# A prefix sum of V on TensorE instead of on VectorE and DMA transposes, in a Taylor-attention plus ternary-FFN kernel

## The chip, the cores and the metric

The kernel runs on the eight cores of one Trainium2 chip. Each core gets one sample of the batch (2048 rows of 1024) and works alone; no data passes between cores. The metric is the device time in microseconds of the slowest core. PE is TensorE, DVE is VectorE, ACT is ScalarE, SP is the SyncE queue, which here issues the DMA transposes, and POOL is GpSimd.

## The reference, cut to what matters

```python
xn  = layernorm(x)                                  # [2048, 1024] per core
q, k = xn @ Wq.T, xn @ Wk.T                         # 16 heads x 16 features
v   = xn @ Wv.T                                     # 16 heads x 64
qf, kf = taylor_exp(q), taylor_exp(k)               # [1, x/2, x(x)x/(4 sqrt 2)]
A   = tril(qf @ kf.T)                               # per head, 2048 x 2048
y   = A @ v
y   = y * rsqrt(mean(y*y) + 1e-5) * g
out = x + y @ Wo.T + gelu(xn @ tern(W1).T + b1) @ tern(W2).T + b2
```

With s = q.k, an entry of A is 1 + s/4 + s²/32, which is (s/√32 + 4/√32)² + 0.5. The kernel squares and accumulates only the first term. The constant 0.5, under the causal mask, adds 0.5 times the running sum of V over the sequence to each row of y. This prefix sum is what the change touches.

## The kernel before, in words

One core's program runs in stages. First LayerNorm, while ACT sums the absolute values of W1 and W2 as they are loaded. Then the q, k and v projections on PE (L715), copied out of PSUM by ACT (L616). Then the prefix sum of V, then attention over eight pairs of heads, then the output projection, the ternary weights and the FFN.

**The prefix sum before.** V lies in `v_tm` with the sequence on partitions. SP transposes it by DMA into `vTc` (L215, sixteen transposes), so that the sequence runs along the free dimension. DVE scans it in place with 128 `tensor_tensor_scan` of 128x128 (L401), each tile starting from the last column of the one before. For each pair and each of 16 tiles of 128 rows SP transposes the piece back by DMA into `cumvT` (L230, 128 transposes in all). DVE adds 0.5 times that piece when it copies y out of PSUM into `y_tm` (L435).

**A pair's loop.** For pair p, PE first writes zeros into the four banks of `psY` (L761), each bank after DVE has copied the previous pair's y out of it. For m = 0 to 15, and for each of the two heads, PE computes scores in chunks of up to 512 columns into four buffers `psS` in turn (L778). Chunk i needs the buffer of chunk i-4. Every third chunk is turned by DVE into its square (L464, then L468), the other two by ACT (L649), both into `A_buf`. DVE masks the diagonal block (L479). PE accumulates `A_buf` times V into `psY` (L746, 128x64 results, each with its own weight load). It does so for m-1 after the scores of m. After m = 4, 8, 12 and at the end a bank is closed (L753) and DVE copies its four tiles out. There are 80 chunks in a pair.

**The head of a pair.** On DVE, from pair 1 on, two memsets of `qh_ext` rows (L445) stand ahead of the chunks; PE's first score waits for both. Behind them come the squares and sums of the previous pair's y (L411, L414) and, from pair 2 on, a reciprocal and sixteen scalings of the pair before that (L421, L427). Only then does DVE take its first chunk, which is chunk 2. Without it PE stops before chunk 6.

**The start of pair 0.** SP's program is in order: it waits for all transposes into `vTc` before it loads the first two heads of q into `qh_ext` (L221), and PE's first score waits for these. DVE's program is in order too: all 128 scans stand ahead of its first chunk.

Of the kernel before, what the change touches and what calls it, by code (L numbers as in the profile page):

```python
# [38 lines left out]
def build_program():  # L39
# [22 lines left out]
    xnT = at("xnT", [128, NT, KD, 128], BF16, 0)  # L62
    vTc = at("vTc", [128, NT, KD, 128], BF16, 32)
    w12_sb = at("w12_sb", [128, 32768], BF16, 32)
# [6 lines left out]
    ajunk = at("ajunk", [128, T], BF16, 72)  # L71
    cumvT = at("cumvT", [128, 2, NT, 128], BF16, 176)
    wv_bf = at("wv_bf", [128, KD, D], BF16, 48)
# [19 lines left out]
    A_buf = at("A_buf", [128, 4, T], BF16, 112)  # L93
    ones_scan = at("ones_scan", [128, T], BF16, 184)
    wk_bf = at("wk_bf", [128, KD, 256], BF16, 188)
# [32 lines left out]
    def S(name):  # L128
        return ctx.enter_context(nc.semaphore(name))
# [16 lines left out]
    sXN = S("sXN"); dXNT = DS("dXNT")  # L146
    sPQ = S("sPQ"); sPE = S("sPE"); dVT = DS("dVT"); sCUM = S("sCUM")
    sEXT = S("sEXT"); sSC = S("sSC"); sPOLY = S("sPOLY"); sPOLYV = S("sPOLYV"); sDM = S("sDM")
    sAV = S("sAV"); sYB = S("sYB"); sYE = S("sYE"); sYT = S("sYT")
    dCVT = DS("dCVT"); sQZ = S("sQZ")  # L150
    dP1L = DS("dP1L"); sP1R = S("sP1R"); sTHR = S("sTHR"); sZL = S("sZL")
# [45 lines left out]
    def sync_stream(e):  # L197
# [6 lines left out]
        for t in range(NT):  # L204
            e.wait_ge(sXN, t + 1)
            if t >= 2:
# [3 lines left out]
                                 transpose=True), t)  # L210
        for t in range(NT):
            e.wait_ge(sPE, 48 if t >= 8 else 33 + t)
            if t >= 2:
                dVT.wait_done(e, t - 2)
            dVT.inc(e.dma_start(out=vTc[:, t, :, :],  # L215
                                in_=blk(v_tm[:, t, :], KD), transpose=True), t)
        dVT.wait_all(e, NT)
        for h in (0, 1):
# [4 lines left out]
        for p in range(8):  # L223
            for t in range(NT):
                if p >= 2:
                    e.wait_ge(sYE, 16 * (p - 2) + t + 1)
                e.wait_ge(sCUM, 8 * (t + 1))
                if 16 * p + t >= 2:
                    dCVT.wait_done(e, 16 * p + t - 2)
                dCVT.inc(e.dma_start(out=cumvT[:, p % 2, t:t + 1, :],  # L230
                                     in_=vTc[:, t, p:p + 1, :],
                                     transpose=True), 16 * p + t)
            for h in (2 * p + 2, 2 * p + 3):
                if h < 16:
                    e.wait_ge(sSC, last_sc_of_pair[p])
                    e.wait_ge(sQZ, 2 * p - 1 if p >= 2 else 1)
                    r0 = 16 * (h % 8)
                    e.dma_start(out=qh_ext[r0:r0 + 16, h % 2, :],
                                in_=qT[r0:r0 + 16, h // 8, :]).then_inc(sEXT, 16)
            if p >= 3:  # L240
                pp = p - 3
                e.wait_ge(sRMc, NT * (pp + 1))
                e.wait_ge(sRMcS, NT * (pp + 1))
                if pp >= 2:
                    dYTT.wait_done(e, pp - 2)
                dYTT.inc(e.dma_start(out=blk(yT[:, pp, :], NT),
                                     in_=y_tm[:, pp % 4, :, :],
                                     transpose=True), pp)
# [95 lines left out]
    def vec_stream(e):  # L344
# [13 lines left out]
        pub(e.memset(ones1_bf[:], 1.0))  # L358
        pub(e.memset(zrow_bf[:], 0.0))
        pub(e.memset(cc(C_ONE), 1.0))  # L360
        pub(e.memset(consts[0:1, C_OR:C_OR + 128], 1.0))
        pub(e.memset(ones_scan[:], 1.0))
        pub(e.memset(cc(C_CBI), BI))
# [4 lines left out]
        pub(e.memset(cc(C_CZ), 0.0))  # L368
        pub(e.memset(cc(C_CO), 1.0))
        fence()  # L370
        for tp in range(0, NT, 2):
# [18 lines left out]
            for t in (tp, tp + 1):  # L390
                e.wait_ge(sLNrc, t + 1)
                e.tensor_scalar(xn_tm[:, t, :], u_sb[:, t % 2, :],
                                cc(C_RC + t), None, ALU.mult).then_inc(sXN, 1)
        for t in range(NT):
            dVT.wait_done(e, t)
            for c in range(KD):
                sl = vTc[:, t, c, :]
                init = 0.0 if t == 0 else vTc[:, t - 1, c, 127:128]
                if t > 0:
                    e.wait_ge(sCUM, 8 * (t - 1) + c + 1)  # L400
                e.tensor_tensor_scan(sl, sl, ones_scan[:, 0:128], init,  # L401
                                     ALU.add, ALU.mult).then_inc(sCUM, 1)
        pvk = [0]
# [26 lines left out]
        def evac_t(p, t):  # L430
            if t == 0 and p >= 4:
                dYTT.wait_done(e, p - 4)
            e.wait_ge(sYB, 4 * p + t // 4 + 1)
            dCVT.wait_done(e, 16 * p + t)
            e.scalar_tensor_tensor(  # L435
                y_tm[:, p % 4, t, :], cumvT[:, p % 2, t, :], 0.5,
                psY[:, 128 * t:128 * (t + 1)],
                ALU.mult, ALU.add).then_inc(sYE, 1)

# [253 lines left out]
    def ten_stream(e):  # L693
# [24 lines left out]
        e.wait_ge(sPE, 48)  # L718
        e.wait_ge(sCUM, 8)

# [36 lines left out]
        for p in range(8):  # L757
            for b in range(4):
                if p > 0:
                    e.wait_ge(sYE, 16 * (p - 1) + 4 * (b + 1))  # L760
                e.matmul(psY[:, 512 * b:512 * (b + 1)], zrow_bf[:],  # L761
                         v_tm[0:1, 0, 0:512], start=True, stop=False)
            for m in range(NT):
                chs = strip_chunks(m)
# [130 lines left out]
```

## Time and profile before

| | us |
|---|---|
| median of 2 runs | 1515.3 |
| lowest, highest | 1505.99, 1524.61 |
| the profiled execution, its time | 1505.63 |
| its span on core 0, the slowest | 1503.9 |
| spans of the other cores | 1483.6 to 1501.7 |

The profiled execution is read on core 0. Times in it count from the first instruction of that core; its span is 1.7 us shorter than the time of the execution. The stages on core 0 are: LayerNorm and weight sums to about 217 us, projections to 298 us, the wait for the prefix sum to about 326 us, the eight pairs to 773 us, and the rest to the end.

### The profile page before, as it was taken

How to read it: one execution, taken by the hardware profiler on the slowest of the kernel's cores; microseconds unless marked ns; L12 is line 12 of the kernel's file. 1: busy time of each engine (PE TensorE's matmuls, PEld its weight loads, DVE VectorE, ACT ScalarE, POOL GpSimd, SP SyncE). 2: the span in 40 equal slices, each digit the busy share in tenths (PEclk: the TensorE clock that was granted, in tenths of full speed). 3: DMA queues.
4: the chain of work that ended last, by engine and by line, in shares of the span. 5: the costliest groups of instructions: out<-in, count | busy, mean ns of one | idle time of the engine just before them, and what ended most of it. 6: DMA issues, size and time to landing. Idle time of an engine off the chain costs nothing.

```text
span 1503.9 us, 19832 instructions; the slowest of 8 cores (1483.6 to 1503.9 us)
## 1 busy us (share of the span) xinstructions
PE 925.5 (62%) x5528; PEld 433.0 (29%) x5608; DVE 597.4 (40%) x1406; ACT 528.8 (35%) x886; POOL 93.2 (6%) x155
## 2 busy tenths in 40 slices
PE   0000049936767657667543953888898506899995
PEld 0000014414334324334221321333343203344442
DVE  2222100687777777776762535222222100001000
ACT  1555333336657767667660211333333200000000
POOL 1111100000000000000001000111111100010010
PEclk9999999959879879779776986999999857999998
DMA  9878970330000010110217844545445564564662
GB/s 193 238 251 266 220 145 1 63 68 9 12 18 9 12 32 7 28 31 7 43 27 168 287 177 164 163 149 162 157 161 164 171 183 114 147 141 115 174 152 36
DMA packets 157670, 175.39 MB, mean 117 GB/s; under 512 B 77440, under 2 KB 128640, under 8 KB 153472
## 3 DMA queue, kind: packets, MB, share of 16 engines
q0 software_dynamic: 24928, 97.53, 23.6%
q1 hardware_dynamic: 132640, 76.60, 20.0%
q8 instruction: 52, 0.85, 0.2%
q14 instruction: 50, 0.41, 0.1%
HBM read 119.56 MB, written 41.94 MB: 107 GB/s over the span
## 4 chain that ended last, share of the span: by engine, by line
PE 32%; DMA 31%; DVE 18%; issue 11%; ACT 3%; POOL 1%; SPq 1%; DVEq 1%; another core or an unknown queue 0%; PEld 0%; POOLq 0%; ACTq 0%; PEldq 0%
DMA wst<-w2T 10%; PE psS L852 8%; PE psS L778 6%; DMA p1st<-w1T 6%; PE psS L715 5%; PE psY L852 5%; DMA xnT<-xn_tm 4%; DVE pv L464 4%; PE psY L746 4%; DMA hg_ts<-hg_scr 3%; DMA w_sb<-w2t_scr 3%; ACT A_buf L649 2%; PE psS L816 2%; PE psY L816 2%; DVE A_buf L468 2%
## 5 line engine op out<-in xcount | busy, mean ns | idle before, releaser
L649 ACT ACTIVATE A_buf<-psS,consts 128x512 bf16<-128x512 f32 (+3 forms) x427 | 277.7, 712 | 174.3 <-PE psS L778 146.2
L830 PE MATMUL psS<-xnT,w_sb 128*128 128x512 bf16 x1024 | 232.7, 386 | 69.1 <-DVE w_sb L525 39.7
L778 PE MATMUL psS<-qh_ext,kT 128*128 128x512 bf16 (+3 forms) x593 | 181.1, 385 | 149.1 <-DVE A_buf L468 73.3
L852 PE MATMUL psS<-w_sb,hg_ts 128*128 128x512 bf16 x501 | 114.6, 387 | 75.4 <-DMA hg_ts<-hg_scr 71.6
L830 PEld LDWEIGHTS psS<-xnT,w_sb 128*128 128x128 bf16 x1024 | 99.4, 99 | 202.3 <-issue 93.1
L464 DVE TENSOR_SCALAR pv<-psS 128x512 bf16<-128x512 f32 (+3 forms) x213 | 129.5, 608 | 59.9 <-PE psS L778 50.8
L715 PE MATMUL psS<-xnT,wq_bf 128*128 128x512 bf16 x64 | 21.9, 515 | 206.7 <-DMA xnT<-xn_tm 206.7
L682 ACT ACTIVATE hgst<-psS,consts 128x512 bf16<-128x512 f32 x128 | 85.5, 686 | 172.7 <-DMA hg_scr<-hgst 91.4
L778 PEld LDWEIGHTS psS<-qh_ext,kT 128*128 128x128 bf16 x640 | 62.1, 99 | 249.5 <-issue 236.3
L746 PE MATMUL psY<-v_tm,A_buf 128*128 128x64 bf16 x2176 | 119.2, 192 | 18.8 <-DVE A_buf L479 5.6
L746 PEld LDWEIGHTS psY<-v_tm,A_buf 128*128 128x128 bf16 x2176 | 98.7, 97 | 45.7 <-issue 31.4
L852 PE MATMUL psY<-w_sb,hg_ts 128*128 128x512 bf16 x502 | 111.3, 379 | 0.5
L561 DVE TENSOR_SCALAR jw2a<-wst,consts 128x1024 bf16<-128x1024 f32 x32 | 24.1, 753 | 193.2 <-DMA wst<-w2T 193.2
L589 ACT ACTIVATE ajunk<-p1st 128x2048 bf16<-128x2048 f32 x32 | 61.1, 1910 | 109.1 <-DMA p1st<-w1T 55.1
L468 DVE TENSOR_TENSOR A_buf<-pv 128x512 bf16<-128x512 bf16 (+3 forms) x213 | 82.0, 385 | 22.6 <-DVE pv L464 0.6
L852 PEld LDWEIGHTS psS<-w_sb,hg_ts 128*128 128x128 bf16 x512 | 50.5, 100 | 139.5 <-issue 83.1
L551 DVE TENSOR_TENSOR out_sb<-psS,x_re 128x512 f32<-128x512 f32 x16 | 11.1, 692 | 178.4 <-PE psS L852 178.4
L401 DVE TENSOR_TENSOR_SCAN vTc<-vTc,ones_scan 128x128 bf16<-128x128 bf16 x128 | 47.8, 456 | 77.6 <-DMA vTc<-v_tm 77.6
L715 PEld LDWEIGHTS psS<-xnT,wq_bf 128*128 128x128 bf16 x64 | 7.5, 121 | 220.5 <-issue 217.3
L852 PEld LDWEIGHTS psY<-w_sb,hg_ts 128*128 128x128 bf16 x512 | 50.0, 98 | 60.5
L715 PE MATMUL psS<-wv_bf,xnT 128*128 128x512 bf16 x250 | 54.9, 379 | 0.3
L551 DVE TENSOR_TENSOR out_sb<-psY,x_re 128x512 f32<-128x512 f32 x16 | 11.1, 692 | 99.4 <-PE psY L852 99.4
(96 smaller groups left out, 707.3 us busy)
## 6 DMA issues: line engine op xcount, KB each, us to landing
p1st<-w1T POOLq DMA_DIRECT2D x16, 1024.0 KB, 7.9
p1st<-w2T POOLq DMA_DIRECT2D x16, 1024.0 KB, 8.2
wst<-w1T POOLq DMA_DIRECT2D x16, 1024.0 KB, 8.6
wst<-w2T POOLq DMA_DIRECT2D x32, 512.0 KB, 4.7
hg_scr<-hgst SPq DMA_DIRECT2D x128, 128.0 KB, 2.4
hg_ts<-hg_scr SPq DMA_DIRECT2D x32, 512.0 KB, 9.1
x_roll<-x SPq DMA_DIRECT2D x16, 512.0 KB, 6.0
out<-out_sb SPq DMA_DIRECT2D x16, 512.0 KB, 6.0
```

The source lines that it names most:

```text
L401: e.tensor_tensor_scan(sl, sl, ones_scan[:, 0:128], init, ALU.add, ALU.mult).then_inc(sCUM, 1)
L464: pub(e.tensor_scalar(pv[:, slot, 0:w], psS[idx % 4][:, 0:w], SC, BI, ALU.mult, ALU.add))
L468: e.tensor_tensor(A_buf[:, gs % 4, t0:t0 + w], pv[:, slot, 0:w], pv[:, slot, 0:w], ALU.mult).then_inc(sPOLYV, 1)
L589: e.activation(ajunk[:], p1st[:, i % 2, :], AF.Abs, accum_out=cc(col)).then_inc(sP1R, 1)
L649: e.activation(A_buf[:, gs % 4, t0:t0 + w], psS[idx % 4][:, 0:w], AF.Square, bias=cc(C_CBI), scale=cc(C_CSC)).then_inc(sPOLY, 1)
L682: e.activation(hgst[:, i % 2, :], ps[:], AF.Gelu, bias=consts[:, C_B1 + j:C_B1 + j + 1]).then_inc(sHGs, 1)
L715: mm = e.matmul(ps[:], lhsT, rhs, start=(c == 0), stop=(c == KD - 1))
L746: e.matmul(psY[:, 128 * t + 64 * hi:128 * t + 64 * hi + 64], A_buf[:, gs % 4, 128 * t:128 * (t + 1)], v_tm[:, m, h * E:(h + 1) * E], start ...
L778: e.matmul(psS[idx % 4][:, 0:w], kT[:, h // 8, m * 128:(m + 1) * 128], qh_ext[:, hi, t0:t0 + w], start=True, stop=True).then_inc(sSC, 1)
L816: e.matmul(ps, yT[:, c, t * 128:(t + 1) * 128], wo_bf[:, c, dh * 512:(dh + 1) * 512], start=(c == 0), stop=False)
L830: mm = e.matmul(ps[:], w12_sb[:, c * FF + j * 128:c * FF + j * 128 + 128], xnT[:, 4 * tb:4 * tb + 4, c, :], start=(c == 0), stop=(c == KD ...
L852: mm = e.matmul(ps, hg_ts[:, k % 2, j, (ts % 2) * 128:(ts % 2) * 128 + 128], w12_sb[:, j * D + dh * 512:j * D + (dh + 1) * 512], start=(j ...
```

## The change

The prefix sum moves to PE. Two constant 128x128 matrices are made: `oneh`, all 0.5, and `tril05`, the mask times 0.5. At the head of each pair, behind the zeros and ahead of the first score, PE accumulates into `psY`, for each tile mm_ of V and each row tile t from mm_ to 15, one matmul of 128 columns: with `tril05` for t = mm_, with `oneh` for t above it. That is 136 matmuls for each pair and 1088 in all. The transposes into `vTc`, the scans, and the transposes into `cumvT` are gone. DVE's copy out of `psY` becomes a plain `tensor_copy`. SP loads the first two heads of q once the eight q projections are copied out. PE's wait for the first scans becomes one for `tril05`. In the diff, renamed semaphores and tile declarations are left out.

```diff
@@ sync_stream
-        for t in range(NT):
-            e.wait_ge(sPE, 48 if t >= 8 else 33 + t)
-            if t >= 2:
-                dVT.wait_done(e, t - 2)
-            dVT.inc(e.dma_start(out=vTc[:, t, :, :],
-                                in_=blk(v_tm[:, t, :], KD), transpose=True), t)
-        dVT.wait_all(e, NT)
+        e.wait_ge(sPE, 8)
         for h in (0, 1):
             r0 = 16 * (h % 8)
             e.wait_ge(sQZ, 1)
             e.dma_start(out=qh_ext[r0:r0 + 16, h % 2, :],
                         in_=qT[r0:r0 + 16, h // 8, :]).then_inc(sEXT, 16)
         for p in range(8):
-            for t in range(NT):
-                if p >= 2:
-                    e.wait_ge(sYE, 16 * (p - 2) + t + 1)
-                e.wait_ge(sCUM, 8 * (t + 1))
-                if 16 * p + t >= 2:
-                    dCVT.wait_done(e, 16 * p + t - 2)
-                dCVT.inc(e.dma_start(out=cumvT[:, p % 2, t:t + 1, :],
-                                     in_=vTc[:, t, p:p + 1, :],
-                                     transpose=True), 16 * p + t)
             for h in (2 * p + 2, 2 * p + 3):
@@ vec_stream
+        pub(e.memset(oneh[:], 0.5))
-        pub(e.memset(ones_scan[:], 1.0))
+        fence()
+        e.tensor_scalar(tril05[:], tril_bf[:], 0.5, None,
+                        ALU.mult).then_inc(sVM, 1)
@@
-        for t in range(NT):
-            dVT.wait_done(e, t)
-            for c in range(KD):
-                sl = vTc[:, t, c, :]
-                init = 0.0 if t == 0 else vTc[:, t - 1, c, 127:128]
-                if t > 0:
-                    e.wait_ge(sCUM, 8 * (t - 1) + c + 1)
-                e.tensor_tensor_scan(sl, sl, ones_scan[:, 0:128], init,
-                                     ALU.add, ALU.mult).then_inc(sCUM, 1)
@@ evac_t
             e.wait_ge(sYB, 4 * p + t // 4 + 1)
-            dCVT.wait_done(e, 16 * p + t)
-            e.scalar_tensor_tensor(
-                y_tm[:, p % 4, t, :], cumvT[:, p % 2, t, :], 0.5,
-                psY[:, 128 * t:128 * (t + 1)],
-                ALU.mult, ALU.add).then_inc(sYE, 1)
+            e.tensor_copy(y_tm[:, p % 4, t, :],
+                          psY[:, 128 * t:128 * (t + 1)]).then_inc(sYE, 1)
@@ ten_stream
         e.wait_ge(sPE, 48)
-        e.wait_ge(sCUM, 8)
+        e.wait_ge(sVM, 1)
@@ the head of each pair, behind the zeros
+            for mm_ in range(NT):
+                for t in range(mm_, NT):
+                    e.matmul(psY[:, 128 * t:128 * (t + 1)],
+                             tril05[:] if t == mm_ else oneh[:],
+                             v_tm[:, mm_, 128 * p:128 * (p + 1)],
+                             start=False, stop=False)
```

## Rows read from the trace of the kernel before

**Rows 1.** The page: engines' busy us; one group: busy us, mean ns, idle before.

```profile
PE 925.5 (62%) x5528; PEld 433.0 (29%) x5608; DVE 597.4 (40%) x1406; ACT 528.8 (35%) x886; POOL 93.2 (6%) x155
...
L746 PE MATMUL psY<-v_tm,A_buf 128*128 128x64 bf16 x2176 | 119.2, 192 | 18.8 <-DVE A_buf L479 5.6
```

**Rows 2.** Waits of PE: engine line <- waited for: us, times, longest us.

```profile
PE psS L778 <- DVE A_buf L468: 73.3, 67, 8.2
...
PE psS L778 <- DVE qh_ext L445: 30.6, 7, 4.4
...
PE psS L778 <- DMA qh_ext<-qT: 16.6, 1, 16.6
```

**Rows 3.** Windows, pair 7: engines' busy us (x), granted clock, DMA share, GB/s.

```profile
715.30:773.00 57.70, 36.55 (x351) 20.34 (x356) 44.13 (x122) 35.51 (x59) 0.00 (x0) 0.85 0.13 25
```

**Rows 4.** Timeline around pair 0's start: start us, us, engine, line, tiles, [idle before].

```profile
295.94 0.59 ACT L616 CAST v_tm<-psS 128x512 bf16<-128x512 f32 x1 [1.14 <-PE psS L715]
297.67 0.59 ACT L616 CAST v_tm<-psS 128x512 bf16<-128x512 f32 x1 [1.14 <-PE psS L715]
...
298.51 1.02 PE L761 MATMUL psY<-v_tm,zrow_bf 1*128 1x512 bf16 x4 [0.93 <-DVE vTc L401]
...
301.77 24.16 DVE L401 TENSOR_TENSOR_SCAN vTc<-vTc,ones_scan 128x128 bf16<-128x128 bf16 x64 [2.53 <-DMA vTc<-v_tm]
...
325.85 0.67 DVE L464 TENSOR_SCALAR pv<-psS 128x512 bf16<-128x512 f32 x1
...
327.87 2.79 ACT L649 ACTIVATE A_buf<-psS,consts 128x512 bf16<-128x512 f32 x4 [8.24 <-PE psS L778]
...
330.15 0.69 DVE L464 TENSOR_SCALAR pv<-psS 128x512 bf16<-128x512 f32 x1 [0.51 <-PE psS L778]
```

**Rows 5.** Timeline at the head of pair 3.

```profile
482.84 1.98 PE L761 MATMUL psY<-v_tm,zrow_bf 1*128 1x512 bf16 x4
...
484.58 1.76 DVE L445 MEMSET qh_ext<- 32x2048 bf16 x1 [0.48 <-DVE y_tm L435]
...
489.22 2.48 PE L778 MATMUL psS<-qh_ext,kT 128*128 128x512 bf16 x5 [4.40 <-DVE qh_ext L445]
...
495.35 0.69 DVE L464 TENSOR_SCALAR pv<-psS 128x512 bf16<-128x512 f32 x1
...
496.72 0.59 PE L778 MATMUL psS<-qh_ext,kT 128*128 128x512 bf16 x1 [5.02 <-DVE A_buf L468]
...
497.40 4.02 ACT L649 ACTIVATE A_buf<-psS,consts 128x512 bf16<-128x512 f32 x6 [5.09 <-PE psS L778]
```

**Rows 6.** Timeline at the head of pair 1.

```profile
370.53 1.99 PE L761 MATMUL psY<-v_tm,zrow_bf 1*128 1x512 bf16 x4
...
379.96 0.68 DVE L464 TENSOR_SCALAR pv<-psS 128x512 bf16<-128x512 f32 x1
...
382.00 2.68 ACT L649 ACTIVATE A_buf<-psS,consts 128x512 bf16<-128x512 f32 x4 [3.03 <-PE psS L778]
```

**Rows 7.** Windows: clock after the projections, then from two starts of dense PE work.

```profile
298.30:301.00 2.70, 1.02 (x4) 0.30 (x4) 0.94 (x3) 0.00 (x0) 0.00 (x0) 0.94 0.52 98
...
440.60:447.60 7.00, 6.28 (x46) 2.64 (x46) 4.93 (x13) 5.60 (x9) 0.00 (x0) 0.76 0.12 24
...
554.30:561.30 7.00, 6.63 (x45) 2.60 (x45) 5.24 (x12) 5.54 (x8) 0.00 (x0) 0.59 0.13 27
```

**Rows 8.** Timeline of PE and its weight loads in pair 7, full clock.

```profile
754.69 0.38 PE L778 MATMUL psS<-qh_ext,kT 128*128 128x512 bf16 x1
...
758.11 0.69 PE L746 MATMUL psY<-v_tm,A_buf 128*128 128x64 bf16 x18
...
757.89 0.78 PEld L746 LDWEIGHTS psY<-v_tm,A_buf 128*128 128x128 bf16 x18
```

**Rows 9.** Groups by line and shape: busy us, mean ns, idle before.

```profile
L435 DVE SCALAR_TENSOR_TENSOR y_tm<-cumvT,psY 128x128 bf16<-128x128 bf16 x128 | 28.2, 282 | 13.0 <-PE psY L753 13.0
...
L464 DVE TENSOR_SCALAR pv<-psS 128x128 bf16<-128x128 f32 x21 | 6.1, 290 | 7.6 <-PE psS L778 7.5
```

## What the change will do to the time

> **What bounds the kernel now.** I read the page first. PE is busy in 62% of the span [rows 1], so no engine bounds the whole; each stage has to be asked what it waits for. The list of PE's waits shows three that belong to attention: for the q rows of `qh_ext` by DMA, once, 16.6 us; for the memsets of `qh_ext` at seven pair heads, 30.6 us; for squares from DVE, 73.3 us in 67 waits [rows 2]. Then the timeline of the start of pair 0. ACT begins to copy the last projection out at 297.67 us. PE writes zeros at once, from 298.51, and then has nothing to do: DVE scans, and its first chunk is at 325.85 [rows 4]. The 27 us from 298.5 on are the price of the prefix sum where it stands now. Within pairs it is nearly free: no wait of DVE for `cumvT` appears among its waits.
>
> The next place is the head of a later pair, since the change puts its work there. At pair 3 the zeros begin at 482.84 and last 1.98 us. PE then waits for the memsets that start at 484.58, issues five scores from 489.22, and waits 5.02 us for DVE, until 496.72. DVE is at its own head work up to 495.35, when it takes its first chunk [rows 5]. So between 484.8 and 495.35 PE has 10.6 us in which it does 2.5 us of scores. This idle time recurs in six pairs (2 to 7; from the first memset to the first chunk all have 10.8 us, to 0.1). Pair 1 has no scaling work and DVE is back at 379.96, with the zeros issued from 370.53 for 1.99 us, so 7.5 us after them [rows 6]. The last pair has 57.7 us and ends at 773 [rows 3]. Last I read the granted clock, because PE's new work falls there.
>
> **Part 1, what is removed: the wait before pair 0.** After the change PE goes from the projections into the zeros (298.51 to about 299.4) and into 136 matmuls. In the 2.7 us behind the projections the clock is 0.94 of full in the mean [rows 7], though PE stands idle in the second half of them; with no idle gap I take the full 2.4 GHz. What does one 128-column matmul with its own load cost? No row has them in a stream. Below it are 18 matmuls of 64 columns, each with its load, in 0.69 us of which the last one's own 0.19 us [rows 1] goes off: 0.50/17 = 29 ns [rows 8]. Above it are the projections, eight 512-column matmuls for each of ACT's copies, which start at 295.94 and 297.67: 1.73/8 = 216 ns [rows 4]. On the line between, 128 columns cost 29 + (216-29) x 64/448 = 56 ns, and 136 of them 7.6 us. The upper bound is a load that hides behind nothing. Loads stream at (0.78-0.10)/17 = 40 ns [rows 8], so 96 ns and 13.1 us. I take 56, since the 64-column row hides a whole load in 29 ns.
>
> A rule that speaks against this stands in the Trainium skill, TensorE: Matmul & The Clock Gate, section Back-to-back issue gap: a sustained stream of load and matmul pairs needs about 81 ns for each 128-column matmul. By it the block would be 11.0 us at full clock, and the whole sum, worked out as below, about +4 us instead of a gain. The row of 29 ns for 64 columns disagrees in kind, and no row here shows 128 columns.
>
> So the block ends at 299.4 + 7.6 = 307.0. The first score takes 0.38 us at full clock [rows 8] and reaches ACT 0.1 us later; ACT's four first units last 2.79 us as they do at 327.87 [rows 4]; ACT is ready for its fifth at 310.3. Before, it began the fifth at 327.87. That is 17.6 us earlier. DVE would start at 307.9 instead of 325.85, 17.9 us earlier. The smaller counts: **-17.6 us**.
>
> **Part 2, what is added at the heads of pairs 2 to 7.** The block starts when the zeros are through, 484.8 at pair 3. Here the clock stands at half. From nine starts of dense PE work (eight pairs and the output projection) I took windows of 7 us; their mean clocks are 0.59 to 0.76 [rows 7]. With c us at half clock the mean is 1 - c/14, so c is 3.4 to 5.7 us, 4.4 in the mean. At half clock 128 columns take twice the 53 ns, 107 ns. In 4.4 us that is 41 matmuls; the other 95 take 5.3 us. The block lasts 9.7 us (9.2 to 10.4 for the ends of c; 14.5 if the clock never rises) and ends at 494.5. PE's third score then ends at 494.5 + 2 x 0.216 + 0.38 and is with DVE at 495.4. DVE is free at 495.35, so nothing is lost there. ACT loses its head start. It gets its first chunk at 495.0, is through four at 497.8, and begins the fifth 0.4 us after the 497.40 of before [rows 5]. Against that PE comes out of the block at full clock. Before, a pair's first 3.4 to 5.7 us of scores ran at half, each taking 0.59 against 0.38 us [rows 5, 8]. About three of them lie in the chain from square to score to square in that time: 0.6 us back. Net -0.2 us for each of six pairs: **-1.2 us**. The 10.6 us are the cover; what the block has over 9.7 us costs its full length in all seven later pairs.
>
> **Pair 1.** The block starts at 372.45 and ends at 382.1. ACT begins its fifth unit at 385.4 instead of 382.00 [rows 6]: +3.4, less 0.6: **+2.8 us**. Pair 0 gets the same 0.6 us for a clock that is up where it was at half: **-0.6 us**.
>
> **Part 3, what is smaller.** The copy out of `psY` was 282 ns; the nearest plain op on PSUM of that shape is 290 ns [rows 9], so +1 us over 128 of them at most, mostly beside other work. I take 0. The waits for `cumvT` were never last. The `ones_scan` memset goes (2048 columns take 1.76 us [rows 5]) and two small ops come. It stood ahead of LayerNorm, a stage whose chain is the loading of W1 and W2 and ACT's sums behind it. I take 0, with -1.8 as the bound. SP's queue loses 144 transposes. The `qh_ext` loads of later pairs and `yT` wait for scores and for ACT, not for the queue. The first two q rows now leave SP during the projections. All behind 773 us starts from the last copies of pair 7 and moves with them.
>
> **Sum:** -17.6 - 0.6 + 2.8 - 1.2 = -16.6 us. From the profiled execution's 1505.6 that is **1489 us**. The median of the two runs is 1515.3, 10 us above that execution; I forecast for an execution like the profiled one. About 2% is what can be told from no change here, so -1.1% counts as within it.
>
> **The rivals.**
>
> *The clock pays more (faster).* If the clock rises soon, counted from the zeros at 482.84, c from the block's start is about 2.4 us, the block 8.7 us, and ACT's lag of 0.4 us is gone. If DVE's wait for a half-clock score in that stretch is gone as well (0.5 us [rows 4]), each of eight pairs gives about 0.9 us more: -7, so 1482 us. For it: PE was busy through the zeros. Against it: the units of ACT follow each other without gaps there, so it may be ACT that paces.
>
> *Loads do not hide.* A matmul then costs up to 96 ns. Halfway, at 76 ns, the block has 11.6 us at the heads (1.9 over) and 10.3 at pair 0 (2.7 over): 7 x 1.9 + 2.7 = +16, so 1505. At 96 ns it has 13.5 and 13.1 us: 7 x 3.8 + 5.5 = +32, so 1521. For it: no row shows this shape. Against it: the 64-column row. By the Trainium skill's rule above, this rival would stand at 1509.
>
> *The clock stays at half through the block (slower than before).* The block has 14.5 us at pairs 1 to 7, scores start cold, ACT begins its fifth unit at 484.8 + 14.5 + 0.7 + 2.8 = 502.8 instead of 497.4, 5.4 us late, six times; pair 1 is 8.4 late; with -17.6 that is +23, so 1529 us. It decides from a block of about 12 us on, where seven times the excess eats the gain. For it: half clock at every head now. Against it: all nine dense starts rose within 5.7 us.
>
> **How the numbers follow.** Forecast 0.62 (own range 1483 to 1497), the faster rival 0.18, loads 0.10, clock 0.06, the rest 0.04. The time is the forecast's, 1489. Down to 1476 and up to 1510 leaves out the upper half of the loads rival, the clock rival and part of the rest, under 2 in 10. Faster by over 2% needs more than the faster rival, or runs of before as long as the longer of the two shown: 0.12. Slower by over 2% needs 1536 and thus more than either slow rival: 0.03. Within 2%: 0.85.
>
> **What the new profile would show.** The block's matmuls at about 56 ns spacing at full clock and 107 at half; pair 0's first DVE chunk near 308; the block's end near 10 us after the zeros; PE's wait for `qh_ext` memsets gone; pairs 2 to 7 as long as before within 1 us and pair 1 about 3 us longer; pair 7's end near 756. I am wrong if the spacing is over 70 ns, if the clock stays at half through a block, or if the pairs' bodies change length for another reason.

## The result and the profile after

| | before | after |
|---|---|---|
| median, us | 1513.2 (10 runs) | 1492.5 (11 runs) |
| lowest, highest | 1504.9, 1540.3 | 1489.1, 1504.5 |
| span of core 0 in the profiled execution | 1503.9 | 1492.7 |
| from ACT's last projection copy to the last four copies of y, core 0 | 475.20 | 457.76 |

The ratio of the two kernels is 0.988, with a 95% interval of 0.984 to 0.993: 1.2% faster, some 18 us, and within 2%. In some executions one die shows a lower granted clock; the ratio leaves those out, and the medians do not. The forecast was 1489 us, 1.1% faster, for an execution like the profiled one; that one took 1494.5 us after, against 1505.6 before.

The span of the one profiled execution fell by 11.2 us, the attention stretch in it by 17.4. The rest is not the change's. From these last copies of y on, core 0 needs 731.0 us before (1503.9 - 772.87) and 735.7 after (1492.7 - 756.97); over all eight cores this tail, which the change doesn't touch, has 727.6 us in the mean before and 728.2 after. What lies ahead of the stretch has 291.5 and 291.8 us. So the attention stretch of core 0 is what I compare from here on, unless the text names other cores. It repeats well: over the eight cores it is 474.7 to 476.2 us before and 456.7 to 458.4 after, 475.3 and 457.7 in the mean.

The next table cuts this stretch where DVE starts the last four copies of each pair's y (L435, later L412; one row in the timelines of core 0). "First" runs from ACT's last projection copy to the end of pair 0.

| kernel | first | 1 | 2 | 3 | 4 | 5 | 6 | 7 | sum |
|---|---|---|---|---|---|---|---|---|---|
| before | 73.2 | 56.1 | 56.2 | 57.6 | 59.2 | 55.7 | 58.0 | 59.1 | 475.2 |
| after | 55.0 | 58.2 | 56.1 | 57.7 | 59.1 | 56.2 | 56.8 | 58.8 | 457.8 |
| e1_no_block | 47.8 | 56.2 | 56.1 | 57.9 | 59.3 | 56.2 | 57.3 | 60.0 | 450.8 |
| e2_double_block | 64.5 | 66.2 | 62.4 | 65.5 | 66.3 | 62.6 | 65.2 | 66.1 | 518.8 |
| e3_spread | 50.1 | 58.5 | 59.3 | 60.7 | 61.2 | 59.0 | 59.5 | 62.2 | 470.4 |
| e4_before_plus_heads | 73.2 | 58.5 | 56.0 | 57.2 | 58.5 | 55.6 | 58.6 | 59.5 | 477.1 |
| e5_pair0_spread | 50.3 | 57.8 | 56.1 | 57.9 | 58.8 | 55.3 | 56.8 | 58.7 | 451.7 |
| e6_pool_memset | 55.0 | 58.3 | 55.9 | 56.5 | 58.1 | 55.7 | 56.3 | 58.1 | 453.9 |
| e7_pool_memset_no_block | 47.6 | 52.0 | 52.5 | 52.9 | 54.7 | 52.0 | 53.1 | 54.6 | 419.5 |
| e8_pool_part_spread | 49.0 | 55.1 | 52.1 | 54.5 | 55.8 | 52.7 | 53.4 | 55.3 | 427.8 |
| e9_half_zero_block | 53.4 | 56.4 | 56.6 | 57.4 | 59.2 | 55.6 | 57.0 | 59.1 | 454.7 |
| e10_pool_k4 | 50.1 | 52.9 | 52.2 | 52.8 | 54.7 | 52.4 | 53.4 | 54.9 | 423.4 |
| e11_pool_spread_all | 49.1 | 54.9 | 54.9 | 55.7 | 57.1 | 55.3 | 55.7 | 56.6 | 439.2 |

After against before: -18.2 in the first stretch, +2.1 in pair 1, -1.3 in pairs 2 to 7 together, -17.4 in all. Now the lines behind each.

**The start of pair 0**, from the timeline of the kernel after (start us, us, engine, line, tiles, idle before it). It answers [rows 4].

```profile
299.21 0.59 ACT L591 CAST v_tm<-psS 128x512 bf16<-128x512 f32 x1 [1.14 <-PE psS L690]
...
300.05 1.02 PE L736 MATMUL psY<-v_tm,zrow_bf 1*128 1x512 bf16 x4 [0.93 <-ACT v_tm L591]
...
301.00 0.23 PE L740 MATMUL psY<-v_tm,tril 128*128 128x128 bf16 x1
...
308.55 0.22 PE L740 MATMUL psY<-v_tm,tril 128*128 128x128 bf16 x1
...
309.08 6.70 ACT L624 ACTIVATE A_buf<-psS,consts 128x512 bf16<-128x512 f32 x10 [9.28 <-remote]
...
309.52 0.69 DVE L439 TENSOR_SCALAR pv<-psS 128x512 bf16<-128x512 f32 x1 [107.26 <-PE psS L759]
```

The last projection copy starts at 299.21 here, 1.5 us later than before, so I count from it. (The trace calls `tril05` `tril`.) The zeros follow, then the block (L740) from 301.00; its last matmul starts at 308.55. That is 7.55 us for 135 steps, 55.9 ns each, at full clock. DVE takes its first chunk 10.3 us after the last projection copy; before it was 28.2 us (325.85 - 297.67).

**The head of pair 3**, which answers [rows 5]:

```profile
469.86 1.76 DVE L420 MEMSET qh_ext<- 32x2048 bf16 x1 [0.48 <-DVE y_tm L412]
...
470.03 0.29 PE L740 MATMUL psY<-v_tm,tril 128*128 128x128 bf16 x1
...
471.71 0.31 PE L740 MATMUL psY<-v_tm,tril 128*128 128x128 bf16 x1
...
479.04 0.22 PE L740 MATMUL psY<-v_tm,tril 128*128 128x128 bf16 x1
...
479.31 0.81 PE L759 MATMUL psS<-qh_ext,kT 128*128 128x512 bf16 x3
...
479.57 2.79 ACT L624 ACTIVATE A_buf<-psS,consts 128x512 bf16<-128x512 f32 x4 [8.72 <-remote]
...
480.63 0.69 DVE L439 TENSOR_SCALAR pv<-psS 128x512 bf16<-128x512 f32 x1
...
482.83 3.35 ACT L624 ACTIVATE A_buf<-psS,consts 128x512 bf16<-128x512 f32 x5 [0.47 <-PE psS L759]
```

The first sixteen matmuls of the block take 1.68 us (470.03 to 471.71), 105 ns each, at half clock. The last one starts at 479.04, so the block has 9.0 us plus the last one's time, and ACT has the first score at 479.57. DVE's first chunk comes 10.77 us after the memset's start, to the hundredth what [rows 5] show (495.35 - 484.58). PE's wait for the memsets, which end at 473.8, has gone; the block lies over them.

**The head of pair 1**, which answers [rows 6]:

```profile
355.45 1.76 DVE L420 MEMSET qh_ext<- 32x2048 bf16 x1 [0.36 <-DVE y_tm L412]
...
355.74 0.29 PE L740 MATMUL psY<-v_tm,tril 128*128 128x128 bf16 x1
...
365.53 0.22 PE L740 MATMUL psY<-v_tm,tril 128*128 128x128 bf16 x1
...
366.08 0.69 DVE L439 TENSOR_SCALAR pv<-psS 128x512 bf16<-128x512 f32 x1 [2.74 <-remote]
...
367.92 4.70 ACT L624 ACTIVATE A_buf<-psS,consts 128x512 bf16<-128x512 f32 x7 [0.19 <-PE psS L759]
```

Here the block ends too late. DVE's first chunk comes 10.63 us after the memset's start, against 7.81 before (379.96 - 372.15).

**What PE still waits for** (engine line <- waited for: us, times, longest us), against [rows 2]:

```profile
PE psS L759 <- DVE A_buf L443: 36.4, 73, 2.1
...
PE psS L759 <- ACT A_buf L624: 20.2, 65, 0.6
```

The waits for the q rows (16.6 us) and for the memsets (30.6) are gone, and that for DVE's squares is halved, from 73.3 to 36.4 us. That for ACT's grew from 13.9 to 20.2. So PE waits some 78 us less. Only 17 us of them became time; in the attention stretch PE is busy for 365.7 us where it was 306.1, and these 60 us are the block's matmuls.

**The groups of the page by line and shape** (busy us, mean ns, idle before), against [rows 1, 9]:

```profile
L740 PE MATMUL psY<-v_tm,oneh 128*128 128x128 bf16 x960 | 76.0, 246 | 0.0
...
L740 PE MATMUL psY<-v_tm,tril 128*128 128x128 bf16 x128 | 28.6, 234 | 0.0
...
L412 DVE CAST y_tm<-psY 128x128 bf16<-128x128 f32 x128 | 28.2, 283 | 11.9 <-PE psY L728 11.9
...
L361 DVE TENSOR_REDUCE consts<-x_roll 128x1 f32<-128x1024 f32 x16 | 18.8, 1211 | 1.0 <-DMA x_roll<-x 1.0
```

The plain copy out of PSUM (L412) has 283 ns where the one with the added tile had 282. The first LayerNorm operation (L361) starts 1.9 us earlier than before, at 9.49 us against 11.37, and the second then waits 1.0 us for x to land. Up to the last projection copy nothing of this is left that shows, as the means above say (291.5 and 291.8 us).

### The profile page after: what moved, and what is told of

Read it like the earlier page. It is cut to its first block, busy times and chain, and to the rows that moved or that the text cites. A ratio compares the mean times of both kernels' runs of the same rounds, so it can differ in the third digit from the quotient of the medians.

```text
span 1492.7 us, 21092 instructions; the slowest of 8 cores (1461.5 to 1492.7 us)
## 1 busy us (share of the span) xinstructions
PE 982.0 (66%) x6615; PEld 504.5 (34%) x6696; DVE 548.2 (37%) x1279; ACT 527.1 (35%) x886; POOL 93.5 (6%) x155
## 4 chain that ended last, share of the span: by engine, by line
DMA 34%; PE 29%; DVE 15%; issue 9%; ACT 4%; another core or an unknown queue 2%; SPq 2%; POOL 1%; PEld 1%; DVEq 1%; PEldq 0%; ACTq 0%; POOLq 0%
DMA wst<-w2T 11%; PE psS L833 8%; DMA hg_ts<-hg_scr 6%; DMA p1st<-w1T 6%; PE psS L690 5%; PE psS L759 5%; DMA xnT<-xn_tm 5%; DVE pv L439 4%; PE psY L721 4%; DMA w_sb<-w2t_scr 3%; ACT A_buf L624 3%; PE psS L797 2%; PE psY L797 2%; DVE A_buf L443 2%
## 5 line engine op out<-in xcount | busy, mean ns | idle before, releaser
L811 PE MATMUL psS<-xnT,w_sb 128*128 128x512 bf16 x1024 | 228.4, 381 | 80.3 <-ACT hgst L657 41.4
L759 PE MATMUL psS<-qh_ext,kT 128*128 128x512 bf16 (+3 forms) x592 | 165.2, 348 | 72.6 <-DVE A_buf L443 36.4
L721 PEld LDWEIGHTS psY<-v_tm,A_buf 128*128 128x128 bf16 x2176 | 97.9, 96 | 45.4 <-issue 30.6
L740 PE MATMUL psY<-v_tm,oneh 128*128 128x128 bf16 x960 | 76.0, 246 | 0.0
L740 PEld LDWEIGHTS psY<-v_tm,oneh 128*128 128x128 bf16 x960 | 72.7, 113 | 0.0
L833 PEld LDWEIGHTS psY<-w_sb,hg_ts 128*128 128x128 bf16 x512 | 50.1, 98 | 60.4
L690 PE MATMUL psS<-wv_bf,xnT 128*128 128x512 bf16 x250 | 54.9, 379 | 0.3
```

Of the source, the lines that this page charges most:

```text
L690: mm = e.matmul(ps[:], lhsT, rhs, start=(c == 0), stop=(c == KD - 1))
L721: e.matmul(psY[:, 128 * t + 64 * hi:128 * t + 64 * hi + 64], A_buf[:, gs % 4, 128 * t:128 * (t + 1)], v_tm[:, m, h * E:(h + 1) * E], start ...
L740: e.matmul(psY[:, 128 * t:128 * (t + 1)], tril05[:] if t == mm_ else oneh[:], v_tm[:, mm_, 128 * p:128 * (p + 1)], start=False, stop=False)
L759: e.matmul(psS[idx % 4][:, 0:w], kT[:, h // 8, m * 128:(m + 1) * 128], qh_ext[:, hi, t0:t0 + w], start=True, stop=True).then_inc(sSC, 1)
L811: mm = e.matmul(ps[:], w12_sb[:, c * FF + j * 128:c * FF + j * 128 + 128], xnT[:, 4 * tb:4 * tb + 4, c, :], start=(c == 0), stop=(c == KD ...
L833: mm = e.matmul(ps, hg_ts[:, k % 2, j, (ts % 2) * 128:(ts % 2) * 128 + 128], w12_sb[:, j * D + dh * 512:j * D + (dh + 1) * 512], start=(j ...
```

## The experiments

The theory: the gain is the wait before pair 0, and it pays the block's 7.6 us there in full; the block costs about 2 us at pair 1 (the forecast had 2.8, this is from the result), and in pairs 2 to 7 it lies under DVE's own work at the head, with almost nothing to spare. The rivals: the block costs time at every head; or the pairs' bodies have slack that takes up a late start; or pairs 2 to 7 stay equal because the removed transposes give back what the block takes.

### The block taken away

```diff
-            for mm_ in range(NT):
-                for t in range(mm_, NT):
-                    e.matmul(psY[:, 128 * t:128 * (t + 1)], ...)
```

> The changed kernel without its 136 matmuls at the head of each pair; the constant 0.5 term is left out of the output. My theory (the block is on the path at pair 0 with its full 7.6 us and at pair 1 with about 2 us, and under DVE's head work in pairs 2 to 7): against the changed kernel the stretch from ACT's last projection copy to pair 1's memset is 7.6 us shorter, pair 1 is about 2 us shorter, pairs 2 to 7 are the same within 0.5 us each, and the whole is about 10 us shorter. Rival (PE's time is missed at every head, since ACT starts its first chunk 5 us later than in the kernel before): pairs 2 to 7 are each at least 2 us shorter and the whole at least 20 us.

Against the kernel after, the first stretch is 7.2 us shorter and pair 1 2.0 us, as the theory has it. Pairs 2 to 7 are not shorter but 2.2 us longer together. So the whole is 7.0 us shorter, not 10. The rival is refuted: the heads of pairs 2 to 7 lose 0.9 us by the block, all six together, where it asked for 2 us or more each. The theory misses what the block gives back, 3.1 us in the bodies, 2.2 net. In e1 DVE's first chunk comes as before and ACT starts 5 us earlier than in the kernel after, so what differs must be in the bodies, and the granted clock there differs. First e1's windows of 10 us from DVE's first chunk in pairs 1 and 2, then the kernel after's for pairs 1 and 3 (busy us of the engines, the granted clock, DMA share, GB/s):

```profile
350.12:360.12 10.00, 7.90 (x49) 3.21 (x50) 7.65 (x19) 6.90 (x11) 0.00 (x0) 0.61 0.00 1
...
409.43:419.43 10.00, 7.74 (x50) 3.01 (x50) 7.69 (x19) 7.24 (x11) 0.00 (x0) 0.67 0.00 1
```

```profile
366.08:376.08 10.00, 7.02 (x52) 3.02 (x51) 7.96 (x18) 8.60 (x13) 0.00 (x0) 1.00 0.01 2
...
480.63:490.63 10.00, 7.45 (x51) 3.07 (x51) 7.38 (x19) 8.43 (x14) 0.00 (x0) 0.83 0.00 1
```

Without the block the clock in these 10 us is 0.61 to 0.75 of full over the seven pairs, with it 0.83 to 1.00. Whether this is the cause was tried in e9, and is read from the eight cores behind it.

### The block twice

```diff
+            for mm_ in range(NT):
+                for t in range(mm_, NT):
+                    e.matmul(psY[:, 128 * t:128 * (t + 1)],
+                             zlhs[:],
+                             v_tm[:, mm_, 128 * p:128 * (p + 1)],
+                             start=False, stop=False)
```

> The changed kernel with the block issued twice, the second time with weights of zeros, which add nothing. Theory (the block fills the cover of pairs 2 to 7 to within a microsecond, so everything beyond it counts in full): +7.6 us at pair 0 and +7.6 us at each of pairs 1 to 7, as the second block runs at full clock; 61 us in all. Rival (the bodies of the pairs have slack that takes up a late start): under 40 us in all.

61.0 us longer in the attention stretch (518.8 - 457.8), and the theory said 61. That the sum agrees so well is in part luck: the first stretch has 9.5 more, where 7.6 were expected (the last section shows where the clock fell there), and the seven others 6.4 to 8.4 each, 7.4 in the mean. The timeline of the head of its pair 3:

```profile
490.93 1.76 DVE L420 MEMSET qh_ext<- 32x2048 bf16 x1 [0.48 <-DVE y_tm L412]
...
501.34 7.76 PE L747 MATMUL psY<-v_tm,zlhs 128*128 128x128 bf16 x136
...
508.94 1.03 PE L766 MATMUL psS<-qh_ext,kT 128*128 128x512 bf16 x4
...
509.86 0.69 DVE L439 TENSOR_SCALAR pv<-psS 128x512 bf16<-128x512 f32 x1 [8.07 <-PE psS L766]
```

The zero-weight block (L747) runs for 7.76 us from 501.34, and DVE, done with its own head work, has its first chunk only at 509.86, 18.9 us after the memset's start instead of 10.8. There is next to no slack behind the head: DVE's first chunk comes 7.4 us later in the mean of pairs 2 to 7, and their bodies are only 0.2 us shorter each.

### The block's matmuls in the m loop

```diff
+                if m >= khead:            # khead = 0
+                    prefix(e, p, m)       # the matmuls of tile m of V
                 if m > 0:
                     emit_av(e, p, m - 1)
```

> The changed kernel with the same matmuls spread: those of tile m of V follow the scores of m instead of standing at the pair's head. Theory (the bodies are paced by the handing over between PE, ACT and DVE and PE stands idle in a fifth of them, but heads of pairs 2 to 7 gain nothing as DVE sets them): pair 0 is about 7.6 us shorter less some 3 us for the body, pair 1 about the same, pairs 2 to 7 each 1 to 4 us longer; the whole 5 to 15 us longer. Rival (bodies have room for all of it): pair 0 7.6 us and pair 1 2 us shorter, the rest equal, the whole 10 us shorter.

12.6 us longer, in the range of the theory: 4.9 us shorter in the first stretch, 0.2 longer in pair 1, 17.3 longer in pairs 2 to 7. The heads gain nothing (DVE's first chunk as in e1), and the 7.6 us of matmuls cost a body 2.5 us (e3 against e1 in pairs 1 to 7: 17.3/7). So, by the block's price at full clock, two thirds of the spread work fall into PE's gaps; the rival, that all of it does, is refuted.

### What is added, without what is removed

```diff
+            for mm_ in range(NT if p >= 1 else 0):
+                ...                        # zlhs weights, as in e2
```

> The kernel before, with a block of 136 matmuls whose weights are zeros (they add nothing) at the heads of pairs 1 to 7: the added part of the change alone, without what it removes. Theory: pair 1 is 2 us longer, pairs 2 to 7 together within 2 us of before, the stretch before pair 1 unchanged; about +1 us in all. Rival (the gain in pairs 2 to 7 that offsets the block comes from the transposes and their waits being gone): pairs 2 to 7 are each 0.5 us or more longer, and the whole is 5 us or more longer.

In the kernel before, the block at the heads of pairs 1 to 7 costs 2.4 us in pair 1 and -0.5 us in pairs 2 to 7 together, 1.9 us in all. The transposes and the added operand of the copy are still there, so their absence is not what offsets the block. Core 0 is the least favourable core here: in its pairs 6 and 7 the clock in the first 10 us from DVE's first chunk is 0.66, and they are 0.5 us longer than before, while on most other cores it is at full there. Over the eight cores the attention stretch is 475.3 us in the mean, with this block and without: +1.9 in pair 1, -1.7 in pairs 2 to 7, -0.1 ahead of them. So what is added costs nothing net, and what is removed gives the whole 17.6 us (475.3 - 457.7).

### The block spread in pair 0 only

```diff
+            khead = 0 if p == 0 else NT
```

> The changed kernel with pair 0's matmuls spread over its m loop as in e3_spread and the block kept at the heads of pairs 1 to 7. Theory (a block costs its length where nothing covers it, and spreading costs about 3 us of body): the stretch up to pair 1's memset is 4.9 us shorter, as e3 had it (51.3 against 56.2), all other pairs as in the changed kernel; the whole about 5 us shorter than the changed kernel. Rival (e3's short first stretch was paid by pair 1): pair 1 is 2 us or more longer than in the changed kernel.

4.7 us shorter in the first stretch (50.3) and 6.1 in all; pair 1 didn't pay for it (57.8 against 58.2). The ratio to the kernel before is 0.986 with an interval of 0.978 to 0.995, which overlaps that of the kernel after; the gain over it is read from the stretch, not from these.

### The cover taken away

```diff
 (DVE, head of the pair)
-                for hs in (0, 1):
-                    e.wait_ge(sSC, last_sc_of_pair[p - 1])
-                    e.memset(qh_ext[b0:b0 + 32, hs, :], 0.0).then_inc(sQZ, 1)
 (GpSimd)
+        for p in range(1, 8):
+            b0 = 32 * ((p - 1) % 4)
+            for hs in (0, 1):
+                e.wait_ge(sSC, last_sc_of_pair[p - 1])
+                e.memset(qh_ext[b0:b0 + 32, hs, :], 0.0).then_inc(sQZ, 1)
```

> The changed kernel with the two memsets of qh_ext at each pair's head moved from DVE to GpSimd. Theory (in pairs 2 to 7 the block lies under DVE's head work of 10.8 us, 3.9 us of which are these memsets, and becomes the limit when they go): DVE is free 3.9 us earlier but gets its first chunk only 0.5 to 1.5 us earlier, since the block ends when it did; the whole 3 to 8 us shorter than the changed kernel, pair 1 the same. Rival (the block is not what DVE would wait for next): DVE takes its first chunk 3 us or more earlier in each of pairs 2 to 7, 20 us in all.

> As e6_pool_memset, without the block, so that the constant 0.5 term is left out of the output. Theory: without the block nothing stands between the earlier DVE and its chunks; pairs 1 to 7 are each 3 to 3.9 us shorter than in e1_no_block, 21 to 27 us in all. Together with e6 this prices the block where its cover is gone: about 3 us for each of pairs 2 to 7 and over 5 us at pair 1, where it costs 0 and 2 us now. Rival (ACT or the row loads hold the head instead): less than 2 us a pair.

e6 is 3.9 us shorter than the kernel after, as the theory has it. DVE's first chunk comes 0.2 to 0.7 us earlier in pairs 2 to 7, 0.4 in the mean, so the block is what it waits for, and the rival is refuted. e7 is 31.2 us shorter than e1. The head of pair 3 in e6, where GpSimd's memsets run from 468.69 and DVE's last four copies of y from 470.70:

```profile
468.69 3.54 POOL L295 MEMSET qh_ext<- 32x2048 bf16 x2 [52.42 <-PE psS L760]
...
470.70 0.88 DVE L417 CAST y_tm<-psY 128x128 bf16<-128x128 f32 x4 [1.08 <-PE psY L729]
...
476.26 2.43 DVE L410 TENSOR_SCALAR y_tm<-y_tm,rinv 128x64 bf16<-128x64 bf16 x16
...
482.20 0.69 DVE L440 TENSOR_SCALAR pv<-psS 128x512 bf16<-128x512 f32 x1 [3.51 <-PE psS L760]
```

DVE is through with its scalings at 478.7 and takes its first chunk 3.5 us after that. And the same head in e7:

```profile
441.22 3.54 POOL L295 MEMSET qh_ext<- 32x2048 bf16 x2 [49.05 <-PE psS L754]
...
443.25 0.88 DVE L417 CAST y_tm<-psY 128x128 bf16<-128x128 f32 x4 [1.08 <-PE psY L729]
...
445.51 2.48 PE L754 MATMUL psS<-qh_ext,kT 128*128 128x512 bf16 x5 [0.66 <-issue]
...
448.80 2.43 DVE L410 TENSOR_SCALAR y_tm<-y_tm,rinv 128x64 bf16<-128x64 bf16 x16
...
451.14 0.68 DVE L440 TENSOR_SCALAR pv<-psS 128x512 bf16<-128x512 f32 x1
```

Now the scores begin at 445.51, and DVE's first chunk follows its scalings at once, 7.9 us after the last four copies began, against 12.1 in e1. With the cover gone the block costs 3.2 to 3.7 us in each of pairs 2 to 7 (e6 against e7) and 6.3 in pair 1, where it cost -0.4 and 2.0 us with it. At the heads alone it is 3.6 to 4.2 us in pairs 2 to 7, about the 3.9 us of memsets that went, and the bodies give some 0.5 us back. So the block was hidden by DVE's head work; it was not small in itself. The theory's figure for e7, 21 to 27 us, was low. The heads gained 4.0 to 4.2 us each, 29 us in all: besides the two memsets (3.5 us) the gaps ahead of them went (0.48 and 0.38 us). The other 2 us lie mostly in the bodies and stay unexplained.

### Both kernels beaten: the block cut to the cover

```diff
+            khead = 0 if p == 0 else 6     # e10: 0, then 2 for pair 1 and 4 for the others
+            for mm_ in range(khead):
+                prefix(e, p, mm_)
```

with GpSimd's memsets as in e6.

> GpSimd memsets as in e6; pair 0's prefix matmuls spread over its m loop; in pairs 1 to 7 those of V's tiles 0 to 5 (81 of 136) at the head and the other 55 in the m loop. Theory: the head block then lasts about 6.6 us, as long as DVE's head work without the memsets; each of pairs 2 to 7 gains about 3 us at the head and gives back 1.2 us in its body (3 us for 136 spread matmuls in e3), pair 0 gains 4.9 us; the whole 14 to 20 us shorter than the changed kernel. Rival (spread matmuls hurt where bodies start earlier and are denser): under 8 us shorter.

> e8_pool_part_spread with fewer matmuls at the head: V's tiles 0 and 1 (31 matmuls) in pair 1, 0 to 3 (58) in pairs 2 to 7, all others in the m loop. Theory (in e8 DVE still gets its first chunk 0.4 to 1.6 us after it is free, 3.1 us in pair 1): pair 1 is 2 us shorter, pairs 2 to 7 each 0 to 1 us shorter at the head less 0.5 us for the 23 more in the body; the whole 0 to 4 us shorter than e8. Rival (with a shorter block the clock is at half where the chunks begin and the body pays): 2 us or more longer than e8.

> GpSimd memsets and all prefix matmuls in the m loop, none at the head. Theory (matmuls in the head's cover are free, those in the body cost about 3 us for 136, as e3 had it against e1): against e7_pool_memset_no_block each pair is about 3 us longer, so the attention stretch is 20 to 25 us longer than e7's 419.5 and 10 to 17 us longer than e8's 427.8. Rival (e8 shows spreading to be nearly free once the head is short): within 6 us of e8.

| kernel | attention stretch, us | median, us | ratio to before, 95% interval |
|---|---|---|---|
| after | 457.8 | 1492.5 | 0.988 (0.984 to 0.993) |
| e8_pool_part_spread | 427.8 | 1458.5 | 0.970 (0.966 to 0.975) |
| e10_pool_k4 | 423.4 | 1459.9 | 0.971 (0.968 to 0.975) |
| e11_pool_spread_all | 439.2 | 1470.7, one run | |

e8 is 30 us shorter than the kernel after, where I expected 14 to 20, and 3.0% faster than the kernel before. Of the 30 us, 6.0 are pair 0's, whose matmuls are spread. The head of its pair 3:

```profile
442.73 0.88 DVE L417 CAST y_tm<-psY 128x128 bf16<-128x128 f32 x4 [0.85 <-PE psY L736]
...
448.29 2.43 DVE L410 TENSOR_SCALAR y_tm<-y_tm,rinv 128x64 bf16<-128x64 bf16 x16
...
451.55 0.81 PE L764 MATMUL psS<-qh_ext,kT 128*128 128x512 bf16 x3
...
452.26 0.69 DVE L440 TENSOR_SCALAR pv<-psS 128x512 bf16<-128x512 f32 x1 [1.54 <-PE psS L764]
```

DVE's first chunk comes 1.5 us after its scalings end and 9.5 us after the last four copies began; the kernel after needed 12.1. Over pairs 1 to 7 the heads gain 24.7 us and the pairs 24.0, so the bodies are 0.1 us longer each than in the kernel after. Against e6, which has the same memsets on GpSimd and nothing spread, they are 0.3 us longer each: that is the price of the 55 spread matmuls, where I had allowed 1.2 us. e10 removes what is left at the heads (DVE's first chunk at 7.9 us again, as without any block) and has 4.4 us less in the stretch, a little more than expected; in the medians, taken on another chip, the two can't be told apart. e11 shows that the part at the head is what pays: with none there, the stretch is 19.7 us longer than in e7 (20 to 25 expected) and 11.4 us longer than in e8, and its rival is refuted.

### The clock or ACT's start

```diff
-            for mm_ in range(NT):
+            for mm_ in range(5):           # zlhs weights: 70 matmuls
```

> The changed kernel with its block replaced by 70 matmuls with weights of zeros (tiles 0 to 4 of V), so that the constant 0.5 term is left out; it tells the clock from ACT's head start. e1_no_block was 1 us longer in pairs 2 to 6 and 1.1 us in pair 7 than the changed kernel, although its ACT starts 5 us earlier. Theory (the block brings the clock up before the chunks begin, which is worth some 0.6 us a pair): the short block of about 6 us ends as the scores of e1 would begin, ACT keeps most of its start, the clock in the first 10 us from DVE's first chunk is above 0.9, and pairs 2 to 7 together are 2 to 5 us shorter than in e1. Rival (the difference is nothing of the clock's): pairs 2 to 7 as in e1 within 1 us.

Inconclusive. Pairs 2 to 7 are together 1.9 us shorter than in e1 (344.9 against 346.8) on core 0, between what the two theories said, and 0.6 us shorter in the mean of the eight cores. And the condition didn't come about: the clock in the first 10 us is 0.66 to 0.83, since PE waits again behind the short block. The window of pair 2:

```profile
422.19:432.19 10.00, 7.66 (x48) 3.18 (x50) 7.52 (x19) 7.03 (x11) 0.00 (x0) 0.66 0.01 2
```

What e9 leaves open, the eight cores of one profile settle: they run the same program, and the clock falls at different times on them. Take pair 3 of the kernel after. On cores 0, 1, 2 and 6 the clock is at half for 3.4 of the first 10 us from DVE's first chunk, and the body lasts 45.4 to 45.5 us. On cores 3, 5 and 7 it is at half for 6.8 of them, and the body lasts 46.4 to 46.5 us. On all seven DVE's first chunk comes 12.1 us after the last four copies began, and ACT begins its fifth unit at the same point to 0.01 us. The whole body of pair 3 on core 0, then the first 10 us and the whole body on core 3:

```profile
480.63:526.14 45.51, 34.21 (x348) 19.99 (x353) 31.16 (x97) 36.02 (x59) 0.00 (x0) 0.94 0.02 4
...
474.75:484.75 10.00, 7.88 (x49) 3.47 (x48) 6.75 (x17) 7.65 (x13) 0.00 (x0) 0.66 0.00 1
474.75:521.15 46.40, 35.81 (x353) 20.63 (x353) 31.14 (x98) 35.95 (x59) 0.00 (x0) 0.89 0.02 4
```

So with the head as it was, more time at half clock makes this body 1.0 us longer. The means of the eight cores over pairs 2 to 7 say the same between kernels:

| kernel | clock in the first 10 us | the six heads, us | the six bodies, us |
|---|---|---|---|
| before | 0.70 | 72.5 | 273.5 |
| e4, before plus the block | 0.94 | 73.2 | 271.1 |
| e1, after without the block | 0.69 | 72.6 | 273.4 |
| e9, 70 matmuls at the head | 0.74 | 72.6 | 272.8 |
| after | 0.94 | 73.2 | 271.3 |
| e7, as e6 without the block | 0.70 | 47.4 | 272.3 |
| e6, memsets on GpSimd | 1.00 | 71.0 | 269.9 |

Of two kernels that differ by the block alone (before and e4, e1 and after, e7 and e6), the one with it has the six bodies 2.1 to 2.4 us shorter, some 0.4 us a pair.

## Why the prediction was right, step by step

**The matmul's price** was the widest unknown, 56 to 96 ns from rows of 64 and 512 columns. It measured 55.9 ns; a load hides behind 128 columns at full clock. The line between two shapes on either side was good to 0.2 ns (it gives 55.7 before rounding). The rule of the Trainium skill (TensorE: Matmul & The Clock Gate, Back-to-back issue gap), 81 ns, doesn't hold here.

**Part 1, -17.6 and -0.6 us** at pair 0: -18.2 us measured. DVE's first chunk comes 17.9 us earlier, to the tenth the figure that I had for DVE, and the body is 0.4 us shorter. e1 shows its two terms: the wait that was removed gives 25.4 us (73.2 - 47.8) and the block takes 7.2 back.

**Part 2, pairs 2 to 7, -1.2 us:** measured -1.3, and -1.5 in the mean of the eight cores. The overlap is as I had it; the close agreement is in part luck, since the two terms were both too large. The block's 9.7 us were right: it lasts 9.2 us at pair 3 and 9.2 to 10.5 over pairs 1 to 7, 9.9 in the mean. DVE's first chunk is unchanged in four pairs and late in the two with the longest blocks, by 0.8 us in pair 5 (10.5 us) and by 0.1 in pair 7 (10.4), +0.9 in all. So the cover ends where I had put it, and the pairs stand on its edge. (I gave all six the same 10.8 us from the first memset to the first chunk; pair 5 has 10.6.) For ACT I had a lag of 0.4 us, and its fifth unit at pair 3 is 0.15 us late. For the clock I had 0.6 us back in each body, and it is 0.4. Which scores give it back is not shown: that it is three half-clock scores at the start was a guess. In pair 3 the clock even fell to half again from 483.4 us on, after 0.8 us in which PE waited, so that pair had little of it.

**Pair 1, +2.8 us:** measured +2.1; the head is 2.8 later and the body 0.7 shorter. The step was wrong in a detail. I wrote that DVE's first chunk is chunk 2 in every pair and that ACT has four units ahead of it. Every third chunk is DVE's by a count that runs on over pairs of 80 chunks, so this holds for pairs 0, 3 and 6; in pair 1 it is the very first chunk. The timeline shows it: DVE at 366.08 is ahead of ACT. So the row at 382.00 [rows 6], which I took for ACT's fifth unit, is its third. The error cost little, since what counts is when the block ends.

**Part 3, zeros:** the copy has 283 ns against 282. The shorter DVE work ahead of LayerNorm and SP's shorter queue moved nothing that shows, as said.

**The rivals.** Loads that don't hide: no, 55.9 ns. The clock at half through the whole block: no, at pair 3 it rose about 3 us after the block's start; what a block beyond the cover costs, e2 shows. The clock pays more: the stretch came out 0.8 us beyond my sum, where this rival asked for 7, and the block at the heads had 9.2 us at the least on core 0, not 8.7.

**The cover** of 10.6 us against a block of 9.7 was the sharpest claim. e2 (7.4 of 7.6 us beyond it), e6 with e7 (3.2 to 3.7 us when 3.9 us of it go), and pairs 5 and 7 of the kernel after bear it out.

## What to carry to other kernels

Work that is moved to another engine costs what it overhangs the wait that engine has at that place; so read, for each repetition of the loop, the length of that wait and who ends it, and price the block against it. The first repetition and the second had other covers than the rest here, and they carried the whole cost. When a block just fits under another engine's work, that work and the block have to be cut together: in pairs 1 to 7, moving the memsets alone gave 4 us, and both gave 24 to 29. A block that keeps PE dense at the head gave the pair 0.4 us back, because the clock was then at full in the body's first 10 us more often.

## What the runs showed of the hardware that I had not expected

A matmul of 128 columns with a fresh 128x128 load of weights streams at 55.9 ns at full clock and 105 ns at half, as if the load were free at either level. By its record, which is rough for this engine, GpSimd clears 32x2048 bf16 in 1.80 us, where DVE needs 1.77.

The clock can fall inside dense work. In e2 the double block of pair 0 runs without a gap, but on core 0 the clock was at half from 298.7 to 302.1 us, and the two blocks take 17.0 us where they take 15.4 on core 5. The same fall stands in six of the eight cores, all but 3 and 5. The window of 8.4 us from the zeros on:

```profile
297.60:306.00 8.40, 8.40 (x114) 7.85 (x113) 0.00 (x0) 0.00 (x0) 0.00 (x0) 0.80 0.01 2
```

PE was busy in all of it; what came before was a wait of 1.0 us between the last projection and the zeros, and dense projections before that. In the kernel after the same wait is 0.9 us long, and the clock stays at full through the block on all eight cores. Why the two differ is open.
